# One eight-column spare matmul ahead of the first product of every expert unit, in a fused attention and two-expert-layer kernel

## Chip, cores and metric

The kernel runs on one core of a Trainium2 chip. The metric is device time in microseconds, as the median of several executions. The profile is of one further execution, and the times inside it count from its first instruction. TensorE is PE in the profile (its weight loads are PEld), VectorE is DVE, ScalarE is ACT, GpSimd is POOL and SyncE is SP.

## What is computed

The reference is two layers, each followed by a residual and a layer norm, over 4096 tokens of width 256. The first has a linear attention and a top-2 mixture of 8 GELU experts (hidden width 1024), the second a top-2 mixture of 8 gated experts (two hidden halves of 1024). Each expert works on at most 1280 tokens. Cut to what the change touches:

```python
# first expert layer, for each expert eid, tok = the tokens routed to it (at most 1280)
h = jax.nn.gelu(xf[tok] @ W1[eid] + b1[eid], approximate=False) @ W2[eid] + b2[eid]
out = out.at[tok].add(gate[:, None] * h)
...
# second expert layer, xb = [8, 1280, 256] gathered token rows
gu = jnp.einsum('ecd,efd->ecf', xb, w12)
g, u = jnp.split(gu, 2, axis=-1)
h = jax.nn.silu(g) * u
yb = jnp.einsum('ecf,edf->ecd', h, w3)
```

## The kernel before

The program runs in stages: attention, routing, the first expert phase E1 (`expert_phase` with `glu` false), a bridge with the layer norm and the logits of the second router (`Between`), routing again, and the second expert phase E2 (`glu` true).

An expert phase has 8 experts of 5 units each, 40 units, and a unit is 256 gathered token rows. The order on every engine is written out by hand, with semaphores between the engines; no scheduler and no planner moves anything. `experts` calls `unit` on each engine; the first four units of an expert are a loop on the chip, so that the program text holds fewer units than run.

A float32 product is made of three passes of the TensorE format float32r, since both operands are held as a high and a low part. `product` issues them, high by high (L1380), high by low (L1381), low by high (L1382). Each of the three has its own weight load of 128 columns and streams 256 columns. One unit on TensorE is this sequence:

- **First products** (the first `f` loop of `unit`). Weights `w` are stationary and the unit's transposed rows `xT` stream. 48 matmuls in E1, 96 in E2, where each `f` has two halves. Results go to banks 0 to 3 in turn. Ahead of them stand the wait `s_xl` (the rows' low part is split) and, for each `f`, the wait `s_free` (ACT or DVE has emptied the bank).
- **Transposes** (`turn_rows`, L1373). Four of 128 columns that turn the rows of the next unit, into bank 6. They wait for the gathered rows.
- **Second products** (`second`). The activations `hT` are stationary and `w` streams. 48 matmuls in both phases, into banks 4 and 5.

In the names of the profile a first product reads `bank<-E_xT,ws` and a second product `bank<-ws,E_hT` (or `ws1a`, `ws1b`, the second weight buffer of E1 and of E2). Bank 7 is not used within an expert phase. `keep_busy` (L1431), 512 columns into bank 7, belongs to the bridge, as do the logits of the second router, matmuls of eight columns (L1552).

Where rows lie in memory is set by hand too, by tiles of padding ahead of `xT` and `hT`: with `LINE` at 64 words, `xT` starts at word 48 of a line (`X_AT`) and `hT` at word 16 (`H_AT`).

Of the kernel before, what the change touches and what calls it, by code (L numbers as in the profile page):

```python
# [15 lines left out]
P = 128  # L16
# [8 lines left out]
E = 8  # L25
# [87 lines left out]
def after(eng, sem, count, passed=None):  # L113


    if isinstance(count, int) and count <= 0:
        return
    eng.wait_ge(sem, count)
    if passed is not None:
        eng.sem_inc(passed, 1)  # L120
# [762 lines left out]
def expert_phase(nc, bank, passed, io, tag, glu, X, ysb, s_ys, s_head, kept, IDX, scb, cst, wraw, ws, tail=None):  # L883
# [5 lines left out]
    with ExitStack() as ctx:  # L889
# [36 lines left out]
        def experts(eng, unit, at_expert=None):  # L926

            def one(e, s, last):
                if at_expert:
                    at_expert(e, s, last)  # L930
                width = next_w if last else qw
                if last and glu:
                    for c in range(UPE - 1):
                        unit(e, c, e * UPE + c, s, width, True)
                else:
                    with eng.Fori(0, UPE - 1) as c:
                        unit(e, c, e * UPE + c, s, width, True)
                unit(e, UPE - 1, e * UPE + (UPE - 1), s, 0, not last)
            with eng.Fori(0, E // 2 - 1) as ee:
                for s in range(2):  # L940
                    one(ee * 2 + s, s, False)
            one(E - 2, 0, False)
            one(E - 1, 1, True)
# [423 lines left out]
        @block.tensor  # L1367
        def _(pe):
            def turn_rows(n):
                pe.wait_ge(s_xgn if glu else s_gx, n * UT if glu else n * 16 * UT)  # L1370
                for j in range(UT):
                    for k in range(KD):
                        ins = nc.tensor.transpose(t_ps[:, k, j * P:(j + 1) * P], xgn[:, j, k * P:(k + 1) * P], ident)  # L1373
                ins.then_inc(s_tg, 1)

            def product(out, wts, mov, first, last):

                wh, wl = wts
                mh, ml = mov
                nc.tensor.matmul(out, wh, mh, start=first, stop=False)  # L1380
                nc.tensor.matmul(out, wh, ml, start=False, stop=False)  # L1381
                return nc.tensor.matmul(out, wl, mh, start=False, stop=last)  # L1382

            pe.sem_inc(s_y, 1)
            turn_rows(1)

            def unit(e, c, u, s, width, more):
                w = ws[s]
                pe.wait_ge(s_xl, u + 1)
                for f in range(NF):  # L1390

                    pe.wait_ge(s_free, u * NF + f + 1)
                    for g in range(2 if glu else 1):
                        for k in range(KD):
                            at = k * (2 * HID if glu else HID) + g * HID + f * P
                            ins = product(bank[f % RING][:, g * UW:(g + 1) * UW],
                                          [w[:, a, at:at + P] for a in range(2)],
                                          [xT[:, a, k, :] for a in range(2)], k == 0, k == KD - 1)
                    ins.then_inc(s_hd, 1)
                if more:  # L1400
                    turn_rows(u + 2)
                pe.wait_ge(s_ye, u * UT + UT)
                def second(f, j):

                    pe.wait_ge(s_hl, u * NF + f + 1 + RING)
                    return product(b_y[j][:, 0:D], [hT[:, a, f, j * P:(j + 1) * P] for a in range(2)],
                                   [w[:, a, w2_at + f * D:w2_at + (f + 1) * D] for a in range(2)], f == 0, f == NF - 1)
                if more:
                    for f in range(NF):
                        for j in range(UT):  # L1410
                            ins = second(f, j)
                    ins.then_inc(s_y, 1)
                else:
                    for j in range(UT):
                        for f in range(NF):
                            ins = second(f, j)
                        ins.then_inc(s_y, 1)

            def weights(e, s, last):
                after(pe, s_wl, e * 4 + 4, s_pass_pe)  # L1420
            experts(pe, unit, weights)
            if tail:
                pe.wait_ge(s_sg, UNITS * NF + RING)
                pe.wait_ge(s_ye, UNITS * UT + UT)
                tail.tensor(pe, b2)
# [248 lines left out]
```

## Time and profile before

| | |
|---|---|
| median of 3 runs | 1499.36 us (1498.08 to 1499.55) |
| the profiled execution's own time | 1503.59 us |
| its span, first to last instruction | 1501.8 us |
| mean granted TensorE clock | 0.97 of full |
| PE busy, PEld busy | 95%, 93% of the span |
| DVE, ACT, POOL busy | 67%, 48%, 51% |

Busy shares of PE and PEld are both high because each matmul's record (about 0.28 us) spans its whole passage, while the next starts some 0.11 us after it; the pace of TensorE is therefore read from the starts of the rows, not from their durations. E1 stands in the profile from about 262 to 735 us and E2 from about 799 to 1493 us.

### The profile page before, as it was taken

The page shows a single profiled execution, that of the slowest core. Times are in us where ns is not written, and L with a number is a line of the kernel's source. Part 1 is how long each engine was busy: PE and PEld are TensorE (multiplying, and loading weights), DVE is VectorE, ACT ScalarE, POOL GpSimd, SP SyncE. Part 2 cuts the span into 40 slices and gives each one's busy share as a digit, 9 for nine tenths or more (in the row PEclk, how much of TensorE's full clock was granted, in tenths as well). Part 3 has the DMA queues.
Part 4 walks back from the last instruction along what each step waited for, and adds up shares of the span by engine and source line. Part 5 has one row for each costly group of instructions (what it writes and reads, how often), then busy time and mean ns, then how long its engine had stood idle before and what let it go on. Part 6 is the DMA issues. An engine that isn't in the chain of part 4 may idle for free. (4 is left out here: it accounts for less than half of the span.)

```text
span 1501.8 us, 35841 instructions
## 1 busy us (share of the span) xinstructions
PE 1431.9 (95%) x11738; PEld 1389.9 (93%) x11738; DVE 1011.3 (67%) x2794; ACT 716.9 (48%) x1731; POOL 769.8 (51%) x792
## 2 busy tenths in 40 slices
PE   8999994999999999999966999999999999999997
PEld 7888873999999999999956999999999999999997
DVE  6999986667677667666673556555566656566685
ACT  5677664545555555445553434343334334344353
POOL 3677651566666666665423443344443344343467
PEclk9999995999999999999977999999999999999999
DMA  7121223343343343442522242313323132321442
GB/s 264 43 71 47 62 73 81 98 99 82 63 103 54 93 98 49 106 127 43 139 107 108 32 118 34 112 29 79 69 35 112 28 112 32 113 38 28 107 149 85
DMA packets 63560, 124.79 MB, mean 83 GB/s; under 512 B 14336, under 2 KB 51840, under 8 KB 60416
## 3 DMA queue, kind: packets, MB, share of 16 engines
q0 software_dynamic: 35936, 47.89, 18.8%
q1 hardware_dynamic: 27552, 76.02, 14.0%
q8 instruction: 35, 0.57, 0.2%
q14 instruction: 37, 0.30, 0.1%
HBM read 80.97 MB, written 42.90 MB: 82 GB/s over the span
## 5 line engine op out<-in xcount | busy, mean ns | idle before, releaser
L1015 POOL DMA_INDIRECT E_mg<-meta,IDX x160 | 151.0, 944 | 318.7 <-DVE E_gate L1237 291.0
L1310 DVE TENSOR_TENSOR E_hraw<-E_sg,bank 128x256 f32<-128x256 f32 x320 | 133.5, 418 | 257.2 <-ACT E_sg L1175 201.3
L1022 POOL DMA_INDIRECT acc<-ysb,IDX x150 | 242.9, 1619 | 92.9 <-ACT ysb L1214 53.0
L1380 PE MATMUL bank<-E_xT,ws 128*128 128x256 f32 x960 | 272.5, 284 | 6.0 <-DVE E_xT L1228 5.0
L1381 PE MATMUL bank<-E_xT,ws 128*128 128x256 f32 x960 | 271.6, 283 | 0.0
L1382 PE MATMUL bank<-E_xT,ws 128*128 128x256 f32 x960 | 271.6, 283 | 0.0
L1321 DVE TENSOR_TENSOR E_hT<-E_hraw,E_hT 128x256 fp32r<-128x256 f32 x640 | 260.2, 417 | 0.0
L1317 DVE CAST E_hT<-E_hraw 128x256 fp32r<-128x256 f32 x640 | 206.3, 322 | 63.4 <-ACT E_hraw L1178 42.8
L1175 ACT ACTIVATE E_sg<-bank 128x256 f32<-128x256 f32 x320 | 117.0, 382 | 257.5 <-PE bank L1382 253.9
L1380 PEld LDWEIGHTS bank<-E_xT,ws 128*128 128x128 f32 x960 | 185.8, 194 | 7.6 <-issue 5.8
L1381 PEld LDWEIGHTS bank<-E_xT,ws 128*128 128x128 f32 x960 | 182.2, 190 | 0.0
L1382 PEld LDWEIGHTS bank<-E_xT,ws 128*128 128x128 f32 x960 | 182.1, 190 | 0.0
L1380 PE MATMUL bank<-ws,E_hT 128*128 128x256 f32 x640 | 180.8, 283 | 0.0
L1380 PE MATMUL bank<-E_xT,ws1b 128*128 128x256 f32 x640 | 179.9, 281 | 0.1
L1382 PE MATMUL bank<-E_xT,ws1b 128*128 128x256 f32 x640 | 180.0, 281 | 0.0
L1381 PE MATMUL bank<-E_xT,ws1b 128*128 128x256 f32 x640 | 179.9, 281 | 0.0
L1381 PE MATMUL bank<-ws,E_hT 128*128 128x256 f32 x640 | 177.3, 277 | 0.0
L1382 PE MATMUL bank<-ws,E_hT 128*128 128x256 f32 x640 | 177.2, 277 | 0.0
L1178 ACT ACTIVATE E_hraw<-bank,E_b 128x256 f32<-128x256 f32 x320 | 140.8, 472 | 49.9 <-PE bank L1382 38.6
L1010 POOL DMA_INDIRECT E_xg<-acc,IDX x80 | 81.1, 1014 | 105.0 <-ACT E_xgn L1157 91.9
L1380 PEld LDWEIGHTS bank<-E_xT,ws1b 128*128 128x128 f32 x640 | 122.7, 192 | 0.0
L1010 POOL DMA_INDIRECT E_xg<-xn,IDX x80 | 83.7, 1046 | 72.1 <-PE bank L1373 36.1
(229 smaller groups left out, 3922.6 us busy)
## 6 DMA issues: line engine op xcount, KB each, us to landing
wraw<-in_w_ffn SPq DMA_DIRECT2D x8, 3072.0 KB, 11.2
wraw<-in_w_moe SPq DMA_DIRECT2D x8, 2048.0 KB, 12.5
acc<-x SPq DMA_DIRECT2D x32, 128.0 KB, 1.7
xn<-xn SPq DMA_DIRECT2D x32, 128.0 KB, 1.7
acc<-X POOLq DMA_DIRECT2D x4, 1024.0 KB, 8.3
acc<-X SPq DMA_DIRECT2D x8, 512.0 KB, 4.2
X<-acc SPq DMA_DIRECT2D x7, 512.0 KB, 5.0
X<-in_x SPq DMA_DIRECT2D x3, 1024.0 KB, 11.7
```

Source lines behind the costliest of these rows:

```text
L1010: nc.gpsimd.indirect_dma_start(out=xg[:, j, :], out_offset=None, in_=row_dram, in_offset=at_slots(u, j)).then_inc(s_gx, 16)
L1015: nc.gpsimd.indirect_dma_start(out=mg[:, j, :], out_offset=None, in_=meta_dram, in_offset=at_slots(u, j)).then_inc(s_gm, 16)
L1022: nc.gpsimd.indirect_dma_start(out=acc_dram, out_offset=at_slots(u, j), in_=ysb[:, j, :], in_offset=None, compute_op=ALU.add).then_inc(s_y ...
L1175: nc.scalar.activation(sg[:, f % RING, :], ps[:, 0:UW], ACT.Silu).then_inc(s_sg, 1)
L1178: nc.scalar.activation(hraw[:, f % RING, :], ps[:, 0:UW], ACT.Gelu, bias=b1[:, bass.ds(e * NF + f, 1)]).then_inc(s_sg, 1)
L1310: V.tensor_tensor(hraw[:, f % RING, :], sg[:, f % RING, :], bank[f % RING][:, UW:2 * UW], ALU.mult).then_inc(s_hm, 1)
L1317: V.tensor_copy(hT[:, 0, f, :], hraw[:, f % RING, :]).then_inc(s_hh, 1)
L1321: V.tensor_tensor(hT[:, 1, f, :], hraw[:, f % RING, :], hT[:, 0, f, :].bitcast(F32), ALU.subtract).then_inc(s_hl, 1)
L1380: nc.tensor.matmul(out, wh, mh, start=first, stop=False)
L1381: nc.tensor.matmul(out, wh, ml, start=False, stop=False)
L1382: return nc.tensor.matmul(out, wl, mh, start=False, stop=last)
```

## The change

One matmul is added at the start of `unit` on TensorE, after the wait for the unit's rows and ahead of the first `f`. Its stationary operand is the first 128 columns of the unit's weights, the same that the first product loads next, and it streams the first `E` (8) of those columns into the first eight columns of bank 7. Nothing reads that result.

```diff
             def unit(e, c, u, s, width, more):
                 w = ws[s]
                 pe.wait_ge(s_xl, u + 1)
+                nc.tensor.matmul(bank[7][:, 0:E], w[:, 0, 0:P], w[:, 0, 0:E], start=True, stop=True)
                 for f in range(NF):
 
                     pe.wait_ge(s_free, u * NF + f + 1)
```

It runs once in each unit, 40 times in E1 and 40 times in E2.

On TensorE, at the start of the first unit of E1, the program of before and of the change differ as follows (ISA and REGISTER_ALU are waits and counters of the sequencer; from here on only line numbers differ until the next unit):

```order
 L936 UNCONDITIONAL_BRANCH
 L936 ISA
-L1392 ISA
+L1390 MATMUL bank7<-ws0 128x8
+L1393 ISA
 L1380 MATMUL bank0<-E1_xT,ws0 128x256
 L1381 MATMUL bank0<-E1_xT,ws0 128x256
```

The spare stands between the loop's branch and the wait for a free bank, and nothing else on TensorE has moved.

On TensorE, at the start of the first unit of E2, the changed program reads:

```order
1338 L936 UNCONDITIONAL_BRANCH
1339 L936 ISA
1340 L1390 MATMUL bank<-ws 128x8
1341 L1393 ISA
1342 L1380 MATMUL bank<-E_xT,ws 128x256
1343 L1381 MATMUL bank<-E_xT,ws 128x256
1344 L1382 MATMUL bank<-E_xT,ws 128x256
```

The place is the same as in E1. No other engine's program changes, and no DMA.

## Rows read from the trace of the kernel before

**Rows 1.** The page, parts 1, 2 (40 slices) and 4 (chain by line).

```profile
PE 1431.9 (95%) x11738; PEld 1389.9 (93%) x11738; DVE 1011.3 (67%) x2794; ACT 716.9 (48%) x1731; POOL 769.8 (51%) x792
...
PEclk9999995999999999999977999999999999999999
...
PE bank L1381 14%; PE bank L1380 14%; PE bank L1382 14%; PE bank L1373 1%; POOL out L1062 1%; DMA out<-X 0%; ACT X L1188 0%; POOL wraw L1043 0%; DMA E_mg<-meta,IDX 0%; POOL E_xg L1010 0%; ACT E_xraw L1142 0%; POOL E_rs L1036 0%; ACT E_xgn L1157 0%; POOL E_mg L1015 0%; DVE E_xT L1228 0%
```

**Rows 2.** Busy time of each engine in a window inside E2.

```profile
core 0: us, PE busy (x) PEld busy (x) DVE busy (x) ACT busy (x) POOL busy (x), PEclk, DMA share, GB/s
...
900.00:1000.00 100.00, 100.00 (x863) 100.00 (x862) 59.45 (x166) 38.90 (x84) 41.27 (x36) 1.00 0.27 62
```

**Rows 3.** Waits of PE in E1, window 290 to 745: total, times, longest.

```profile
PE bank L1380 <- ACT E_hraw L1178: 2.4, 5, 0.7
```

**Rows 4.** Timeline of PE, one E2 unit: start, duration, line, operation, count.

```profile
822.42 0.28 PE L1380 MATMUL bank<-E_xT,ws 128*128 128x256 f32 x1
...
833.74 0.60 PE L1373 MATMUL bank<-cst,E_xgn 128*128 128x128 f32 x4
834.09 0.37 PE L1380 MATMUL bank<-ws,E_hT 128*128 128x256 f32 x1
...
839.63 0.28 PE L1380 MATMUL bank<-E_xT,ws 128*128 128x256 f32 x1
```

**Rows 5.** Timeline of PE, first and last of 71 units whose first products start slow.

```profile
278.77 0.28 PE L1380 MATMUL bank<-E_xT,ws 128*128 128x256 f32 x1
...
1459.07 0.28 PE L1380 MATMUL bank<-E_xT,ws1b 128*128 128x256 f32 x1
```

**Rows 6.** Timeline of PE, E1 at a stall and three units on.

```profile
328.30 0.39 PE L1380 MATMUL bank<-E_xT,ws1a 128*128 128x256 f32 x1 [0.33 <-ACT E_hraw L1178]
...
331.15 0.60 PE L1373 MATMUL bank<-cst,E_xg 128*128 128x128 f32 x4
331.50 0.36 PE L1380 MATMUL bank<-ws1a,E_hT 128*128 128x256 f32 x1
...
337.24 0.29 PE L1380 MATMUL bank<-E_xT,ws1a 128*128 128x256 f32 x1
...
342.70 0.60 PE L1373 MATMUL bank<-cst,E_xg 128*128 128x128 f32 x4
343.06 0.37 PE L1380 MATMUL bank<-ws1a,E_hT 128*128 128x256 f32 x1
...
348.59 0.28 PE L1380 MATMUL bank<-E_xT,ws1a 128*128 128x256 f32 x1
...
354.26 0.60 PE L1373 MATMUL bank<-cst,E_xg 128*128 128x128 f32 x4
```

**Rows 7.** Timeline of PE, E2's last unit and the second products before it.

```profile
1470.67 0.36 PE L1380 MATMUL bank<-ws1b,E_hT 128*128 128x256 f32 x1
...
1476.40 0.29 PE L1380 MATMUL bank<-E_xT,ws1b 128*128 128x256 f32 x1
...
1487.31 0.28 PE L1380 MATMUL bank<-ws1b,E_hT 128*128 128x256 f32 x1
```

**Rows 8.** Timeline of PE, the last 24 first products after another stall in E1.

```profile
619.24 0.39 PE L1380 MATMUL bank<-E_xT,ws 128*128 128x256 f32 x1
...
622.17 0.38 PE L1373 MATMUL bank<-cst,E_xg 128*128 128x128 f32 x2
```

**Rows 9.** Timeline of PEld, loads of eight-column matmuls: one load, then two merged.

```profile
760.09 0.19 PEld L1552 LDWEIGHTS bank<-wrg,E_b 128*128 128x128 f32 x1
760.09 0.30 PEld L1552 LDWEIGHTS bank<-wrg,E_b 128*128 128x128 f32 x2
```

**Rows 10.** Timeline of PE, E2's first unit, its transposes and second products.

```profile
816.53 0.60 PE L1373 MATMUL bank<-cst,E_xgn 128*128 128x128 f32 x4
816.88 0.37 PE L1380 MATMUL bank<-ws,E_hT 128*128 128x256 f32 x1
```

## The prediction, made blind

> **What bounds the kernel now.** I read the page first: TensorE and its weight loads are busy for 95% and 93% of the span, and 42% of the chain that ended last lies on the three lines of `product` [rows 1]. Since matmul records overlap, I then looked for anything else that could bound the expert phases. In a window inside E2, PE and PEld are busy without a gap, the granted clock is full, and DVE, ACT and POOL are at 59%, 39% and 41% [rows 2]. In E1 PE waited only 2.4 us, 5 times, for ACT to empty a bank [rows 3]. So in both phases TensorE's own pace sets the time, and a matmul added there lies on the path unless it changes the pace.
>
> The pace itself is read from starts. In one steady unit of E2 the 96 first products take 833.74 - 822.42 = 11.32 us, 0.118 us each. The second products take 839.63 - 834.09 = 5.54 us; their first step is a long 0.2 us after the transposes, and the other 47 go at 0.113 us [rows 4]. Both kinds are 128x256 matmuls with a 128-column load each. So one shape runs at two paces, 4% apart, and which of them a stretch has isn't a matter of its operands: in E1 the same two kinds swap. After a stall the second products that start at 331.50 take 5.74 us to 337.24, and the first products from 337.24 take 5.46 us to 342.70. One unit later it is 5.53 us (343.06 to 348.59) and 5.67 us (348.59 to 354.26) [rows 6]. E2's end shows the same swap: 5.73 us for second products, then 10.91 us for 96 first products [rows 7].
>
> I went through the timeline of PE for all 80 units to see what chooses the pace, and found that it is chosen at the start of a stretch and then kept until something breaks the stream:
> - First products that follow fast second products directly start slow, in all 71 such units [rows 5].
> - First products that follow slow second products directly become fast, in all 7 such units, from 337.24 to 1476.40 [rows 6, 7].
> - Second products that follow the four transposes are fast in 71 of 78 units. The 7 slow ones all follow first products that turned fast midway, as at 328.30. Where the first products were fast from their start on, or from the rise of the clock on in E2's first unit, the second products came out fast too, in all 7 units (343.06 is one, 816.88 with 822.42 - 816.88 = 5.54 us another) [rows 4, 6, 10].
> - After a stall inside a stretch it can be either. The 24 matmuls after the stall at 328.30 took 2.85 us to the transposes, the 24 after that at 619.24 took 2.93 us [rows 6, 8].
>
> **The change, part by part.** One matmul per unit is added at exactly the handover from second to first products.
>
> Its own price. It streams almost nothing, but it needs a load of 128 columns, and the load of the first product behind it must follow. The logits' eight-column matmuls show that: the second load adds 0.30 - 0.19 = 0.11 us [rows 9]. The bounds are 0.09 us from below (four transposes of 128 columns in 834.09 - 833.74 = 0.35 us [rows 4]) and 0.118 us from above, a full place at the slow pace. I take 0.11, since that row has the same form. For 78 units this is 8.6 us. The first unit of each phase runs while the clock is granted at half [rows 1], where I take twice as much, 0.44 us for the two. Sum: +9.0 us, bounds 7.4 to 9.7. Nothing hides it: the loads leave no gap [rows 2].
>
> The Trainium skill (TensorE: Matmul & The Clock Gate, "Back-to-back issue gap") has a floor of about 25 ns for matmuls of up to 64 columns, which alone would make 80 spares an estimated 2 us; its own figure for the load of 128 columns (columns / 1.2) is 107 ns, and the row at 0.11 agrees with that one.
>
> What it does to the pace. Now the first product's load runs beside a full 256-column matmul of the other kind. With the spare it runs beside a matmul of eight columns, so nearly alone, as the load after the last transpose does. The stretches that begin after such a break are those behind the transposes, and 71 of 78 of them are fast; direct handovers from a fast stretch give slow 71 times of 71. So the likeliest outcome is that the first products begin fast. As they are then fast from their start on, the second products behind the transposes stay fast (7 of 7 above), and the next unit finds the same state: it repeats itself.
>
> Gain in E2: of 40 units, 37 are slow throughout now and go from 11.32 to 10.91 us, 37 x 0.41 = 15.2 us. The first and the last are fast already. The one at 1459.07 turned fast midway, and I leave 0.2 us for it: 15.4 us.
> Gain in E1: 27 of 40 units are slow throughout, from 5.67 to 5.46 us, 27 x 0.21 = 5.7 us. Six started fast already. Six turned fast midway, 0.1 us each. For the first unit, which is slow after the clock's rise, 0.1 us. Together 6.4 us. I let the stalls of E1 be as long as now.
> Sum: +9.0 - 15.4 - 6.4 = **-12.8 us**. The profiled execution (1503.59 us, span 1501.8) would go to 1490.8. That execution stands 4.2 us above the median, so on the median I forecast 1499.36 - 12.8 = **1486.6 us**.
>
> Other engines: in E2 a unit shortens from 17.21 to 16.91 us, 2%, and the busiest of them is at 59% [rows 2], so none becomes the bound. The spare writes a bank that no one uses in the phase, and so no one waits for it.
>
> **The rivals.**
> *Pure cost.* The first products stay slow and the second ones fast. For it: the direct handover gives slow without exception, the load of the spare still runs beside the last second product with the same stationary columns as now, and stalls show that a fresh start can end slow [rows 8]. Against it: the load ahead of the first product is then nearly alone. It gives +9.0 us, less up to 1 us that some ten units of E1 stand still for anyway: 1508 us. This is the case on the other side, and its point of decision is the first product's pace in E2: at 0.118 us the change loses, and with the price of 0.11 us it would take a gain of a quarter of the 0.41 us to break even there. A sentence of the Trainium skill speaks for this rival: the same page, in "Step-by-step: what each phase is for", says that loading the next weights doesn't take SBUF read bandwidth from the running matmul, and by its gap rule the spacing depends on the columns alone (109 ns here, estimated from N/2.4 + 2.5); then there would be one pace and nothing to gain. The two paces in the rows disagree with that.
> *First products fast, second ones slow.* This is what follows first products that turned fast midway, 7 of 7 times. E2 then gains 15.4 and loses 38 x 0.2 = 7.6 us, E1 gains 6.4 and loses 33 x 0.2 = 6.6 us (5.74 against 5.53 us [rows 6]), and with the +9.0 it ends at 9.0 - 15.4 + 7.6 - 6.4 + 6.6 = +1.4 us: about 1501 us, no change that can be told.
> *Only one phase changes pace.* E2 alone: -15.4 + 9.0 = -6.4 us, 1493 us. E1 alone: +2.6 us, 1502 us.
> *Both slow.* +9.0 and 71 x 0.2 us for the second products: +23 us, 1522 us. Slow first products never had slow second ones behind the transposes.
> *More stalls in E1.* With a faster TensorE the banks could be waited for longer (2.4 us now [rows 3]). All that E1 can gain net is 2 us, so this moves the result by no more.
>
> **How the numbers follow.** A measurement of this kernel tells 0.2%, 3 us, from no change (its three runs lie within 0.1%). Chances: forecast (both stretches fast in both phases) 0.52; pure cost 0.26; first fast and second slow 0.08; E2 alone 0.05; E1 alone 0.03; both slow 0.03; something else 0.03. Faster by over 0.2%: 0.52 + 0.05 + 0.01 = 0.58. Within: 0.08 + 0.03 + 0.01 = 0.12. Slower: 0.26 + 0.03 + 0.01 = 0.30. The forecast's own range is 1482 to 1491 us, from the bounds of the price (-1.6, +0.7) and from a part of E1 or of the stretches after stalls not following (+3), or stalls that shrink (-3). The whole range has to take in pure cost as well, up to 1509 us with the upper bound of the price: 1482 to 1509.
>
> **What the profile of the changed kernel would show.** If the step on the price is right, the first product starts about 0.11 us later behind the last second product than now, and a steady unit of E2 has one more place. If the step on the pace is right, the 96 first products from their first start to the transposes take 10.9 us instead of 11.32, the 48 second ones keep 5.5 us, and the unit repeats every 16.9 us. Pure cost would show 11.3 and 5.5 us and a unit of 17.3 us; the second rival 10.9 and 5.7 us. The prediction is wrong if the start of a stretch isn't what chooses its pace, or if it is chosen by something finer than what runs beside the first load, such as the exact moment at which that load begins, which rows of 0.01 us don't resolve.

## The result, and the profile after

The changed kernel takes 1517.38 us (median of 4 runs, 1514.41 to 1520.55), beside 1498.72 us for the kernel before on the same chip. The ratio is 1.0124, 95% interval 1.0111 to 1.0137. It is 18.7 us slower where 12.8 us less was forecast. The profiled execution grew from a span of 1501.8 us to 1518.8.

The page of the changed kernel, parts 1 and 5:

```profile
PE 1450.9 (96%) x11818; PEld 1410.5 (93%) x11818; DVE 1021.8 (67%) x2794; ACT 728.6 (48%) x1731; POOL 770.4 (51%) x792
...
L1380 PE MATMUL bank<-E_xT,ws 128*128 128x256 f32 x960 | 275.5, 287 | 0.0
```

The 80 spares are there (11818 against 11738 matmuls, [rows 1]). Asked for the waits of PE between 290 and 745 us, the trace has one, and it belongs to the bridge; the waits for ACT in [rows 3] don't occur in this execution. The stalls turn out below not to go with the spare.

```profile
PE bank L1547 <- DVE E_yraw L1361: 0.6, 1, 0.6
```

The timeline of PE over two units of E2, the counterpart of [rows 4]. L1390 is the spare:

```profile
842.71 0.27 PE L1373 MATMUL bank<-cst,E_xgn 128*128 128x128 f32 x1
...
843.07 0.36 PE L1380 MATMUL bank<-ws,E_hT 128*128 128x256 f32 x1
...
848.80 0.17 PE L1390 MATMUL bank<-ws 128*128 128x8 f32 x1
848.84 0.36 PE L1380 MATMUL bank<-E_xT,ws 128*128 128x256 f32 x1
...
860.23 0.28 PE L1373 MATMUL bank<-cst,E_xgn 128*128 128x128 f32 x1
...
860.59 0.36 PE L1380 MATMUL bank<-ws,E_hT 128*128 128x256 f32 x1
...
866.14 0.17 PE L1390 MATMUL bank<-ws 128*128 128x8 f32 x1
866.17 0.36 PE L1380 MATMUL bank<-E_xT,ws 128*128 128x256 f32 x1
...
877.56 0.27 PE L1373 MATMUL bank<-cst,E_xgn 128*128 128x128 f32 x1
```

Three things are to be seen. The first products take 860.23 - 848.84 = 11.39 us, and 11.39 us again in the next unit. The start of each is shown early, beside the spare, so that its first step reads 0.20 us; the other 95 steps are at 0.118. They are slow, as before. The second products take 5.73 us to 848.80 and then 5.55 us (860.59 to 866.14): **they now alternate between slow and fast from unit to unit**, where before they were fast. And a unit in which the paces are those of before, from one transpose to the next, takes 877.56 - 860.23 = 17.33 us against 17.21 [rows 4], so the spare's place costs 0.12 us.

Counted over the whole timeline, first products are slow from the first full-clock matmul on in all 80 units, and second products are slow in 39 (E2's last unit, whose second products stand still several times, is left out of every such count). Before it was 7 units with first products fast from their start, and 8 slow stretches of second products with the last unit of E1, which has no transposes.

Where the 17.0 us between the two spans are can be read from four starts, that of the first and the last expert unit's stretch in each phase. Before:

```profile
265.69 0.58 PE L1380 MATMUL bank<-E_xT,ws 128*128 128x256 f32 x1 [2.52 <-DVE E_xT L1228]
...
728.20 0.28 PE L1380 MATMUL bank<-ws1a,E_hT 128*128 128x256 f32 x1
...
803.22 0.58 PE L1380 MATMUL bank<-E_xT,ws 128*128 128x256 f32 x1 [2.48 <-DVE E_xT L1228]
```

and, with 1487.31 in [rows 7] for the end of E2's first products, the same four after:

```profile
268.80 0.38 PE L1390 MATMUL bank<-ws 128*128 128x8 f32 x1 [2.44 <-DVE E_xT L1228]
...
736.10 0.28 PE L1380 MATMUL bank<-ws1a,E_hT 128*128 128x256 f32 x1
...
811.24 0.37 PE L1390 MATMUL bank<-ws 128*128 128x8 f32 x1 [2.40 <-DVE E_xT L1228]
...
1504.80 0.28 PE L1380 MATMUL bank<-ws1b,E_hT 128*128 128x256 f32 x1
```

| part | before | after | difference |
|---|---|---|---|
| up to the first expert unit | 265.69 | 268.80 | +3.1 |
| E1 up to its last second products | 462.51 | 467.30 | +4.8 |
| bridge and routing, with E1's last stretch | 75.02 | 75.14 | +0.1 |
| E2 up to its last second products | 684.09 | 693.56 | +9.5 |
| the rest | 14.5 | 14.0 | -0.5 |

The first line is not the change's: attention has no spare, and over the profiles of this study E1 begins anywhere from 264 to 269 us. E2's +9.5 is, to 0.2 us, 40 places at 0.12 us (4.8), 18 more slow stretches of second products at 0.19 us (3.4), and stretches of first products that were fast and are not now (the first unit, 13.3 to 13.9 us, and the last, 10.9 to 11.4; 1.1). In E1 the same terms make about 10 us (4.8 for the places, 13 more slow stretches at 0.19, 1.9 for first products that had been fast, 1.0 in the unit in which the clock rises), and the stalls of before are absent, which is 5 us less: the ten stalled stretches of before were together 5.3 us longer than they are at their paces.

Those stalls are not the unchanged kernel's in every execution. The waits for ACT at L1380 are in the profile of before (an execution of 1503.59 us) and in all four profiles that were taken beside a kernel before of 1503.64 us: xT at word 56 and 40, hT at word 24, and two full spares, which has this row although its units are 0.24 us longer:

```profile
PE bank L1380 <- ACT E_hraw L1178: 1.2, 4, 0.5
```

They are in none of the other twelve profiles, the changed kernel's among them, which were taken where the kernel before takes 1498.7 to 1500.4 us; one of these has no spare either (xT at word 32). So they go with the chip or the execution, and the median of 1498.72 us is probably one without them, which no profile of the kernel before confirms. If it has no slow second products either, the change is 80 places at 0.12 us (9.6) and 39 slow stretches at 0.19 (7.4), an estimate of 17.0 us of the 18.7 measured.

### The profile page after: what moved, and what is told of

It is laid out like the page before. It is cut to its first block and busy times, and to the rows that moved or that the text cites. A ratio compares the mean times of both kernels' runs of the same rounds, so it can differ in the third digit from the quotient of the medians.

```text
span 1518.8 us, 35993 instructions
## 1 busy us (share of the span) xinstructions
PE 1450.9 (96%) x11818; PEld 1410.5 (93%) x11818; DVE 1021.8 (67%) x2794; ACT 728.6 (48%) x1731; POOL 770.4 (51%) x792
## 5 line engine op out<-in xcount | busy, mean ns | idle before, releaser
L1380 PE MATMUL bank<-E_xT,ws 128*128 128x256 f32 x960 | 275.5, 287 | 0.0
L1175 ACT ACTIVATE E_sg<-bank 128x256 f32<-128x256 f32 x320 | 121.7, 384 | 259.0 <-PE bank L1382 257.4
L1317 DVE CAST E_hT<-E_hraw 128x256 fp32r<-128x256 f32 x640 | 203.0, 317 | 59.6 <-ACT E_hraw L1178 51.6
L1380 PEld LDWEIGHTS bank<-E_xT,ws 128*128 128x128 f32 x960 | 182.8, 190 | 0.0
L1380 PE MATMUL bank<-ws,E_hT 128*128 128x256 f32 x640 | 181.8, 284 | 0.0
L1380 PE MATMUL bank<-E_xT,ws1b 128*128 128x256 f32 x640 | 181.5, 284 | 0.0
L559 PE MATMUL bank<-A_wsp,A_xT 128*128 128x512 f32 (+2 forms) x576 | 119.3, 343 | 2.9 <-DVE A_xT L451 2.1
```

The source lines that it names most:

```text
L559: ins = nc.tensor.matmul(out, xT[:, n % 2, a, k, :], wsp[:, b, k, part], start=(k == 0 and m == 0), stop=(k == KD - 1 and m == 2))
L1175: nc.scalar.activation(sg[:, f % RING, :], ps[:, 0:UW], ACT.Silu).then_inc(s_sg, 1)
L1317: V.tensor_copy(hT[:, 0, f, :], hraw[:, f % RING, :]).then_inc(s_hh, 1)
```

## The experiments

Theories, in the words that the expectations use. **Count**: an odd number of matmuls in a unit makes the period of two units. **Neighbour** or **company**: what the first load and the matmul beside it read, and how long that one streams, chooses the pace. **Moment**, later called **meeting**: the pace is chosen by when, to a few ns, and at which addresses the loads and the streams of a stretch meet. The prediction's own step is a form of the second: a first load with almost nothing beside it was to start a fast stretch.

Times are medians beside the kernel before on the same chip. The patterns are counted over the timeline of PE, for 80 stretches of each kind; "slow" and "fast" are 0.118 and 0.113 us a matmul.

**Two spares in place of one.**

```diff
                 nc.tensor.matmul(bank[7][:, 0:E], w[:, 0, 0:P], w[:, 0, 0:E], start=True, stop=True)
+                nc.tensor.matmul(bank[7][:, 0:E], w[:, 0, 0:P], w[:, 0, 0:E], start=True, stop=True)
```

> Two eight-column spares in place of one, at the same place. Price: one more place of 0.11 to 0.12 us in each of 80 units, 9.4 us over the changed kernel's price. Count theory (the second products are slow in every other unit because a unit now has an odd number of matmuls, 101 or 149): with an even number again, every unit is alike and all second products take 5.5 us, so the 38 slow ones give back 7.5 us and the time is that of the changed kernel plus 2 us, about 1519 us. Neighbour theory (what the load and the matmul beside it read at the handover chooses the pace): the second spare has the same neighbours as the first product had behind one spare, so first products stay slow and the second ones alternate: 1527 us. Moment theory (the pace is chosen by the exact moment, to a few ns, at which the first loads of a stretch fall): any pattern; one that differs from both of these, first products fast above all (10.9 us in E2), would speak for it alone.

Measured: 1512.66 us, ratio 1.0093 (1.0057 to 1.0128), less than with one spare. The pattern has a period of three units in both phases: slow and slow, fast and slow, fast and fast (first and second products). First products are fast in 53 units, second ones slow in 52. Count falls: an even number did not make the units alike. Neighbour falls too, for first products behind the second spare are not always slow. First products can be fast behind a short spare, but not always.

**A spare of 256 columns.**

```diff
-                nc.tensor.matmul(bank[7][:, 0:E], w[:, 0, 0:P], w[:, 0, 0:E], start=True, stop=True)
+                nc.tensor.matmul(bank[7][:, 0:UW], w[:, 0, 0:P], w[:, 0, 0:UW], start=True, stop=True)
```

> The spare streams 256 columns instead of 8, same operands and bank. Its place costs 0.113 to 0.118 us instead of 0.110 to 0.12, so the price is about the same, 9.4 us. Neighbour theory: the first product's load again runs beside a full matmul that streams weights, as before the change, so the second products should be fast in all units and the first ones slow: 1499 + 9.4 = 1508 us. Count theory: still an odd number of matmuls, so second products alternate as with eight columns: 1517 us. Moment theory: the shift is some ns other than with eight columns, so the pattern need not be that of eight columns; no time can be named, but each stretch should still be wholly at one of the two paces.

Measured: 1492.81 us (7 runs, 1488.17 to 1494.39), ratio 0.9958 (0.9946 to 0.9971). **It is faster than both kernels.** None of the theories had said so; moment had named no time. The timeline of PE in E2:

```profile
842.47 0.37 PE L1380 MATMUL bank<-ws,E_hT 128*128 128x256 f32 x1
...
848.00 0.28 PE L1390 MATMUL bank<-ws 128*128 128x256 f32 x1
...
882.22 0.28 PE L1390 MATMUL bank<-ws1b 128*128 128x256 f32 x1
882.34 0.29 PE L1380 MATMUL bank<-E_xT,ws1b 128*128 128x256 f32 x1
...
893.24 0.60 PE L1373 MATMUL bank<-cst,E_xgn 128*128 128x128 f32 x4
893.59 0.36 PE L1380 MATMUL bank<-ws1b,E_hT 128*128 128x256 f32 x1
...
899.33 0.28 PE L1390 MATMUL bank<-ws1b 128*128 128x256 f32 x1
```

The first products take 893.24 - 882.34 = 10.90 us, the size that the prediction had wanted, for a place of 0.12 us (882.22 to 882.34). They are fast in 79 of 80 units. Second products are fast in all of E1's units but its last, and in E2 they alternate (848.00 - 842.47 = 5.53 us, 899.33 - 893.59 = 5.74 us).

**Eight columns of xT in place of the weights.**

```diff
-                nc.tensor.matmul(bank[7][:, 0:E], w[:, 0, 0:P], w[:, 0, 0:E], start=True, stop=True)
+                nc.tensor.matmul(bank[7][:, 0:E], w[:, 0, 0:P], xT[:, 0, 0, 0:E], start=True, stop=True)
```

> The eight columns that the spare streams are of xT (word 48 of a line) instead of the weights (word 0); load, bank and place are the same. Neighbour theory: the spare now reads what the first product reads, so the change of operands falls one matmul earlier and the pattern changes (first products fast or second products fast in all units; 1492 to 1508 us). Moment theory: eight columns stream in 3 ns at 2.4 GHz and shift nothing, so the pattern and the time are those of the changed kernel, 1517 us within 3. Count theory: the same, 1517 us.

Measured: 1515.89 us, ratio 1.0114 (1.0082 to 1.0147): within 1.5 us of the changed kernel's time, and its pattern too (first products slow, second ones alternating). What the eight columns read did not matter here.

**The eight-column spare behind the transposes.**

```diff
                 if more:
                     turn_rows(u + 2)
+                nc.tensor.matmul(bank[7][:, 0:E], w[:, 0, 0:P], w[:, 0, 0:E], start=True, stop=True)
                 pe.wait_ge(s_ye, u * UT + UT)
```

> The same spare moved to behind the four transposes, ahead of the second products; none ahead of the first ones. Price the same, 9.4 us. Count theory: odd number of matmuls, so one of the two kinds alternates from unit to unit, about 1517 us. Neighbour theory: the handover from second to first products is that of before, so first products behind fast second ones are slow; second products begin behind a nearly lone load as now and stay fast: 1508 us. Moment theory: the second products start some ns later against the transposes, so their pace may be either, and the first products follow the rule of before (slow behind fast, fast behind slow).

Measured: 1501.07 us (8 runs, 1499.11 to 1507.99), ratio 1.0022 (1.0002 to 1.0041). In E2 every unit has fast first products and slow second ones:

```profile
884.20 0.60 PE L1373 MATMUL bank<-cst,E_xgn 128*128 128x128 f32 x4
884.56 0.25 PE L1402 MATMUL bank<-ws 128*128 128x8 f32 x1
884.67 0.37 PE L1380 MATMUL bank<-ws,E_hT 128*128 128x256 f32 x1
...
890.41 0.29 PE L1380 MATMUL bank<-E_xT,ws1b 128*128 128x256 f32 x1
...
901.31 0.60 PE L1373 MATMUL bank<-cst,E_xgn 128*128 128x128 f32 x4
```

5.74 us and 10.90 us. Here the break with a nearly lone load ends slow, and the rule of the direct handover (fast behind slow) holds again. E1 began so too and changed over to slow first and fast second products after one unit in which the pace turned midway. Neighbour and count had named other patterns; moment had allowed this one, without naming it. The profile is of the shortest of the eight executions (1499.11 us); two took 1507 and 1508, and what pattern they had wasn't recorded.

**Other widths of the spare.** The same line with 128, 192 and 224 columns.

```diff
-                nc.tensor.matmul(bank[7][:, 0:E], w[:, 0, 0:P], w[:, 0, 0:E], start=True, stop=True)
+                nc.tensor.matmul(bank[7][:, 0:128], w[:, 0, 0:P], w[:, 0, 0:128], start=True, stop=True)
```

> The spare ahead of the first products streams 128 columns (8 gave slow first products, 256 fast ones). Company theory, as the 256-column run leaves it (a first load beside a full matmul of weights gives fast first products, beside an almost empty one slow ones): 128 columns stream for half of the load's time, so it should follow one of the two, and 192 columns should lie between: once fast at 128, fast at 192 too. Moment theory: no trend with width need hold. With fast first products the time is between 1490 and 1501 us, with slow ones between 1508 and 1519 us.

> The spare streams 192 columns. Company theory: as at 256 columns, since 80 ns of streaming cover most of the load: first products fast in all units, second products fast in E1 and alternating in E2, 1493 us. Moment theory: the pattern may be that of 256 columns or another; if 128 and 192 don't order between 8 and 256, the width acts only through some ns of shift.

> The spare streams 224 columns of the weights: between 192 (slow first products in 74 of 80 units) and 256 (fast in 78). Meeting theory: its 93 ns of streaming end before the load of 108 does, as at 192, so the first load behind it starts alone and the pattern should be that of 192, slow, about 1508 us. If only the exact shift counts and 256 was a lucky hit, 224 may be anything; a period of three as with 128 would be a sign of that.

Measured, one run each: 1507.96 us at 128 columns and 1508.22 at 192 (before 1500.41), 1508.96 at 224 (before 1498.88). At 128 the period is three again, with first products fast in 27 units (in E1 after some five slower steps) and second ones slow in 26. At 192, after three units at the start of each phase, and at 224 from the start, first products are slow and second ones fast, as before the change. So 192 did not follow 256. This case is the rival that the prediction called pure cost. In E2 at 192 columns:

```profile
874.83 0.25 PE L1390 MATMUL bank<-ws 128*128 128x192 f32 x1
874.92 0.30 PE L1380 MATMUL bank<-E_xT,ws 128*128 128x256 f32 x1
...
886.26 0.60 PE L1373 MATMUL bank<-cst,E_xgn 128*128 128x128 f32 x4
886.61 0.37 PE L1380 MATMUL bank<-ws,E_hT 128*128 128x256 f32 x1
...
892.15 0.25 PE L1390 MATMUL bank<-ws1b 128*128 128x192 f32 x1
```

The unit is 892.15 - 874.83 = 17.32 us, the price of 0.11 us and nothing else.

**The streamed rows at another place in memory, without a spare.**

```diff
-X_AT, H_AT = 48, 16
+X_AT, H_AT = 32, 16
```

> The kernel before, without a spare, with the streamed rows of the first products at word 32 of a line instead of 48 (X_AT = 32, the padding ahead of hT follows). If the two paces come from how the loads and the streams of one stretch meet in memory, moving one operand by 16 words changes the first products' pace or which pace follows which, 5 us or more on the whole time either way; the second products' own operands stay where they were. If the paces are TensorE's alone and don't know addresses, the pattern stays slow first and fast second, 1499 us within 3.

Measured: 1514.55 us beside 1500.41 (one run each). The pace itself is another: in E2 the 96 first products take 11.40 us, 0.1187 us each, and all second products are slow. In E1, at the same addresses of xT and hT within their lines, all second products but the last unit's are fast, so the place alone doesn't fix the pattern.

```profile
875.41 0.28 PE L1380 MATMUL bank<-E_xT,ws 128*128 128x256 f32 x1
...
886.81 0.60 PE L1373 MATMUL bank<-cst,E_xgn 128*128 128x128 f32 x4
887.16 0.36 PE L1380 MATMUL bank<-ws,E_hT 128*128 128x256 f32 x1
...
892.90 0.28 PE L1380 MATMUL bank<-E_xT,ws1b 128*128 128x256 f32 x1
```

Nothing but the address of xT differs, so the slow pace depends on where the streamed rows lie.

**A 256-column spare ahead of the transposes.**

```diff
                 if more:
+                    nc.tensor.matmul(bank[7][:, 0:UW], w[:, 0, 0:P], w[:, 0, 0:UW], start=True, stop=True)
                     turn_rows(u + 2)
```

> A 256-column spare between the first products and the transposes, in the 78 units that have transposes; none ahead of the first products. Price 0.113 to 0.118 us each, 9.2 us. Company theory: nothing changes at the handover from second to first products, so first products behind fast second ones stay slow, and second products still begin behind four transposes and are fast: 1508 us. Moment theory: the transposes and all behind them shift by one place, which need not be a whole number of whatever the pace is locked to, so second products may change pace; where they turn slow the first ones behind them turn fast, 1500 us.

Measured: 1508.59 us beside 1500.41 (one run each). First products slow, second ones fast: pure cost, as the company theory had it; the full spare does not make what follows it fast at any place.

**256 columns of xT.**

```diff
-                nc.tensor.matmul(bank[7][:, 0:E], w[:, 0, 0:P], w[:, 0, 0:E], start=True, stop=True)
+                nc.tensor.matmul(bank[7][:, 0:UW], w[:, 0, 0:P], xT[:, 0, 0, 0:UW], start=True, stop=True)
```

> A spare of 256 columns ahead of the first products, as in the 256-column run that made them fast, but it streams xT instead of the weights, so it is in every operand the same as a first product. Width theory (a full stream at the handover is what makes the first products fast): fast again, 1493 us. Meeting theory (the pace is locked to where in memory and at which moment the loads and streams meet, as the run with xT at word 32 showed that addresses count): the handover from second products is then the direct one of before, one place earlier, and direct handovers from fast second products gave slow first ones 71 times of 71: first products slow behind fast second ones, in E2 97 places at 0.118 us, 1508 us.

Measured: 1507.2 us, ratio 1.0057 (1.0039 to 1.0076). First products are slow in 74 of 80 units, and second ones fast behind them but in E1's last unit, as meeting expected. With the run of 256 columns of weights this shows that at full width what the spare streams does matter. In E2, a spare and 96 first products in 885.99 - 874.56 = 11.43 us, 97 places at 0.118:

```profile
874.56 0.28 PE L1390 MATMUL bank<-E_xT,ws 128*128 128x256 f32 x1
...
885.99 0.60 PE L1373 MATMUL bank<-cst,E_xgn 128*128 128x128 f32 x4
```

**The full spare once more.** No edit against the run of 256 columns of weights.

> The kernel with the 256-column spare once more, for its pattern from execution to execution and for an interval. If the pattern belongs to the program, the profile again has first products fast in 78 of 80 units and second ones alternating in E2, and the time is 1493 us, 0.4% under before. If it also depends on where an execution starts, the count of slow second products differs (each is worth 0.2 us, so 20 of them 4 us), and the times spread by as much, 1488 to 1497 us.

Measured: 1493.77 us (median of eight executions), ratio 0.9963 (0.9949 to 0.9977); one of the eight took 4994 us, for a reason that nothing here shows, and is left out of the ratio. First products are fast in 79 units again. But second products alternate in E1 too, 39 slow in all instead of 20, and the profiled execution took 1493.34 us where the first one had taken 1488.17. So the same program falls into different patterns from one execution to another: 19 more slow stretches at 0.2 us are 3.8 of those 5.2 us. The other six executions of the first run took 1491.8 to 1494.4 us, as these do, so the pattern in its profile is the rarer one.

**Two full spares.**

```diff
+                nc.tensor.matmul(bank[7][:, 0:UW], w[:, 0, 0:P], w[:, 0, 0:UW], start=True, stop=True)
+                nc.tensor.matmul(bank[7][:, 0:UW], w[:, 0, 0:P], w[:, 0, 0:UW], start=True, stop=True)
```

> Two spares of 256 columns of the weights ahead of the first products. One more place in each of 80 units, +9.2 us over one such spare. If a full stream of weights beside the first product's load is what makes the first products fast, they stay fast: 1493 + 9 = 1502 us. Meeting theory: each place in which a load of weights meets a stream of weights shifts the moment of the next load a little, one such place (the direct handover of before) ended slow and two (one full spare) fast, so three need not be fast; slow first products behind fast second ones give 1499 + 18 = 1517 us.

Measured: 1509.52 us beside 1503.64 (one run each). First products are fast throughout in 72 units, second ones alternate:

```profile
880.49 0.28 PE L1390 MATMUL bank<-ws 128*128 128x256 f32 x1
880.73 0.29 PE L1380 MATMUL bank<-E_xT,ws 128*128 128x256 f32 x1
...
891.63 0.60 PE L1373 MATMUL bank<-cst,E_xgn 128*128 128x128 f32 x4
```

10.90 us again, behind two places of 0.12 us. The time rises by 5.9 us over the kernel before, where the fast case expected 3. It expected 9 us over one full spare, whose own gain is 5 to 6 us, so this fits within 2 us. The pattern decides for "a full stream of weights ahead makes the first products fast" at one and two such spares, and against my guess that a third such place might not.

**Finer steps of the addresses, without a spare.**

```diff
-X_AT, H_AT = 48, 16
+X_AT, H_AT = 56, 16
...
+X_AT, H_AT = 40, 16
...
+X_AT, H_AT = 48, 24
```

> The kernel before, without a spare, with xT at word 56 of a line instead of 48; hT stays at word 16. Meeting theory: the moment to which the first products lock moves with their operand's address, so the handover from fast second products, which now always ends slow, may end fast, for no price at all: with first products fast in E2 alone 1484 us, in both phases 1476 us. Or the pace itself changes, as at word 32 (0.1187 us, 1515 us). If only steps of 16 words count, nothing changes: 1499 us within 3.

> The kernel before with xT at word 40 of a line. As with word 56, on the other side: between word 48 (0.1179 us slow, 0.1133 fast) and word 32 (0.1187, never fast). Meeting theory: a pace or an order of paces of its own; 1476 to 1520 us. If steps under 16 words don't count, 1499 us (as word 48) or 1515 us (as word 32) within 3.

> The kernel before with hT, the stationary operand of the second products, at word 24 of a line instead of 16; xT stays at word 48. Meeting theory: the second products' lock moves and with it both handovers, so the second products' pace changes or the first products behind them become fast; 1476 to 1520 us. If the stationary operand's place doesn't count, 1499 us within 3.

Measured, one run each beside 1503.64 us: xT at word 56 takes 1519.48 us, xT at word 40 takes 1503.99, hT at word 24 takes 1512.64. At word 56 first products go at 0.1183 us in all units (11.36 us in E2), and second ones are slow in 60. At word 40 the first products take 11.27 us in E2, 0.1174 each, with second ones slow in 8 units. With hT moved, no stretch of second products is fast; the tiles laid out behind hT, among them the rows that the transposes read, move by 8 words with it (the sum of the two paddings is 88 words instead of 80), so hT alone isn't shown to be the cause. So steps of 8 words count, and none of these places is better than the one that the kernel has.

## Why the prediction was wrong, step by step

- *TensorE's own pace sets the time of both phases.* Right. PE and PEld stay busy (96% and 93% of the span), and the times of the changed kernel and of the full spare follow from places and paces to within some 2 us.
- *The price, 0.11 us each, 9.0 us in all.* Right in kind and close in size: 0.12 us in the unit whose paces are those of before (17.33 against 17.21 us), 0.11 at 192 columns. It is 9 to 10 us of the 18.7.
- *"With the spare it runs beside a matmul of eight columns, so nearly alone... So the likeliest outcome is that the first products begin fast."* This is the step that failed. With 8 columns first products are slow in all units, with 192 and 224 in 74 and 78, with 128 in 53; and in the run with the spare behind the transposes a nearly lone load starts slow second products. I had taken from 71 of 78 fast stretches behind the transposes that a break makes what follows fast. The runs show in its place that a nearly lone first load does not decide the pace (slow in 80 units behind one short spare, fast in 53 behind two), that one or two full streams of weights ahead of the first products do make them fast (79 and 72 units) while a full stream of xT does not (74 slow), and that the address of the stream changes the pace itself. What in a handover makes the choice stays open.
- *Second products stay fast when first ones are fast from their start on (7 of 7).* Not general either: behind the full spare the first products are fast from their start and the second ones alternate in E2, in the repeated run in both phases. Seven cases, most of them from one kind of history, carried too much.
- *"Slow first products never had slow second ones behind the transposes."* True of before and not of the changed kernel, where it happens in every other unit. Those 39 slow stretches against 8 in the profile of before are 31 x 0.19 = 6 us, and 7 us against a kernel before that has none: the largest part of the 9 us that the rival of pure cost (1508 us) lacks of the 1517 measured. The outcome lies between pure cost and "both slow" (1522 us), to which I had given 0.03.
- *The stalls of E1 stay as they are.* Between the two profiles it is wrong by 5 us in the other direction, but the stalls are no property of the kernel (above). The forecast's counts came from the one execution that had them: six of the seven slow stretches of second products behind transposes, and six of the seven stretches of first products that started fast, are E1's, where the stalls are. Why they come in those executions and not in the others stays open.
- *The gain, if the pace changes, 0.41 us a unit in E2 for 96 first products.* Right in size: 11.32 to 10.90 us with the full spare, which also shows that the gain exists and outweighs the price. With the weights as stream, the spare's width decided; with xT as stream, full width did not help.
- The last sentence of the prediction left room for what happened, that the pace is chosen by something finer than what runs beside the first load. That this is the exact moment, its example, is not shown by any run.

An account that fits the runs with full-width spares ahead of the first products, but is argued and not shown: while the second products end and before first ones start, loads of weights run beside streams of weights. Before the change there is one such place (the first product's load beside the last second product), and it ends slow; with one and with two full spares there are two and three, and they end fast; with 256 columns of xT there is one again, and it ends slow. Each kind of pair would pull the moment at which loads begin toward a place of its own, and one pair is not enough to arrive. Open stays why eight columns make second products alternate, and 128 and two spares give a period of three. The starts in the timeline's rows differ by 0.01 us where it matters (the first product is shown at 848.84 with a spare at 848.80 behind slow second products, and at 866.17 with a spare at 866.14 behind fast ones), which is their resolution.

## What to carry to other kernels

Where TensorE is the bound and equal matmuls run at two paces, look at whole stretches and at what state each hands to the next, and treat the choice of pace as unknown: a rule read from a few dozen handovers of one program did not survive a matmul of 0.1 us. Price such an edit at its place, give both paces for every stretch behind it, the untouched ones too, and measure some widths and operands; here 8 columns cost 1.2% and 256 columns of the same weights, at the same price, gained 0.4%. Since the pattern can also differ between executions of one program, judge it by several, and before a rule is taken from stretches behind stalls, see whether the stalls come again in another execution.

## What the runs showed of the hardware

- A matmul with a load of 128 columns of its own costs 0.11 to 0.12 us of place at the full clock whatever it streams: 0.12 with 8 columns (units of 17.33 against 17.21 us), 0.11 with 192 (17.32), 0.12 with 256 (882.22 to 882.34).
- The pace of 128x256 matmuls depends on the word at which the streamed operand starts within a 64-word line: 0.1179 or 0.1133 us with the stream at word 48, 0.1174 at word 40, 0.1183 at word 56, 0.1187 at word 32. The Trainium skill (TensorE: Matmul & The Clock Gate, "Step-by-step: what each phase is for") says that loading the next weights takes no SBUF read bandwidth from the running matmul; these runs, which differ in nothing but the address of the stream, speak against taking that as "costs no time", though none of them tells a load's reads from other reads.
- The state persists for hundreds of us: in the changed kernel the period of two units runs unbroken from 831 us to the end of E2, over 38 units.
- One program can run in different patterns: with the same full spare, second products were slow in 1 unit of E1 in one profiled execution (1488.17 us) and in 20 in another (1493.34 us).
